# New order of the feed-forward part: x products ahead of c1's, upper halves turned elsewhere, last gate in halves of rows, last norm on ScalarE

## What is computed

```python
x = L0_attn_x
x = _layernorm(x + _L0_attn_ref(x, ...))
x = _layernorm(x + _L0_ffn_ref(x, ...))

def step(c, xt):                       # in _L0_ffn_ref, scanned over the 2 halves of x
    ft = jax.nn.sigmoid(xt @ wf.T + c @ uf.T + bf)
    it = jax.nn.sigmoid(xt @ wi.T + c @ ui.T + bi)
    gt = jnp.tanh(xt @ wc.T + c @ uc.T + bc)
    c = ft * c + it * gt
    return (c, None)
c_final, _ = lax.scan(step, c0, x)
h = jnp.tanh(jnp.einsum('tbi,oi->tbo', x, wo) + c_final @ uo.T + bo)
```

## Time and profile before

| | |
|---|---|
| median of 3 runs | 745.36 us (743.22 to 746.38) |
| the profiled execution | 744.35 us |
| its span | 742.2 us |
| PE busy in the span | 688.9 us (93%) |
| DVE, POOL, ACT busy | 69%, 48%, 44% |
| granted clock of PE over the span | 0.978 |

### The profile page before, as it was taken

One profiled execution on the slowest core, in us unless ns is written; L12 is line 12 of the kernel. 1 busy time (PEld: TensorE's weight loads), 2 busy tenths in 40 slices (PEclk: granted clock), 3 DMA queues, 4 the chain that ended last, 5 costly groups with the idle time before them and its releaser, 6 DMA issues. The chain is left out here.

```text
span 742.2 us, 21921 instructions
## 1 busy us (share of the span) xinstructions
PE 688.9 (93%) x9112; PEld 595.7 (80%) x9112; DVE 509.0 (69%) x1096; ACT 323.0 (44%) x708; POOL 357.0 (48%) x462
## 2 busy tenths in 40 slices
PE   6889999999999999999999999999958889999983
PEld 4778888888888888888888888888846678787872
DVE  3655676878688776867678687968773254575758
ACT  5545445354544344454544445354433233434321
POOL 2645564555646554655655464654541224242415
PEclk9999999999999999999999999999997999999997
DMA  8113031222315030121403041221320000010102
GB/s 282 41 36 91 6 87 27 67 42 50 65 28 91 3 91 9 54 49 45 91 2 90 13 80 35 58 55 25 82 68 0 1 1 14 15 44 15 43 7 93
DMA packets 53586, 37.06 MB, mean 50 GB/s; under 512 B 5360, under 2 KB 52080, under 8 KB 53488
## 3 DMA queue, kind: packets, MB, share of 16 engines
q1 hardware_dynamic: 53488, 35.67, 19.1%
HBM read 30.41 MB, written 5.24 MB: 48 GB/s over the span
## 5 line engine op out<-in xcount | busy, mean ns | idle before, releaser
L365 PE MATMUL bank<-xH,wH 128*128 128x256 f32 x480 | 145.7, 304 | 1.4 <-ACT KT L698 1.4
L365 PE MATMUL bank<-xH,wL 128*128 128x256 f32 x480 | 135.1, 281 | 0.0
L365 PE MATMUL bank<-xL,wH 128*128 128x256 f32 x480 | 135.0, 281 | 0.0
L899 DVE TENSOR_TENSOR W<-bank,E 128x512 f32<-128x512 f32 x128 | 82.2, 684 | 54.9 <-PE bank L365 54.4
L365 PEld LDWEIGHTS bank<-xH,wH 128*128 128x128 f32 x480 | 91.0, 190 | 13.3 <-issue 12.6
L365 PEld LDWEIGHTS bank<-xL,wH 128*128 128x128 f32 x480 | 91.4, 191 | 0.0
L365 PEld LDWEIGHTS bank<-xH,wL 128*128 128x128 f32 x480 | 91.0, 189 | 0.0
L698 ACT ACTIVATE QT<-bank 128x512 f32<-128x512 f32 x64 | 38.2, 596 | 106.0 <-PE bank L365 105.9
L365 PE MATMUL bank<-QT,KT 64*128 64x128 f32 x1024 | 74.4, 285 | 0.0
L698 ACT ACTIVATE E<-bank 128x512 f32<-128x512 f32 x128 | 66.1, 605 | 16.6 <-PE bank L387 16.6
L698 ACT ACTIVATE KT<-bank 128x512 f32<-128x512 f32 x64 | 38.3, 598 | 79.4 <-PE bank L365 79.3
(11 more groups left out here) (150 smaller groups left out, 1700.1 us busy)
## 6 DMA issues: line engine op xcount, KB each, us to landing
cB<-scr SPq DMA_DIRECT2D x240, 64.0 KB, 2.9
xt<-in_xT SPq DMA_DIRECT2D x16, 256.0 KB, 3.2
xs<-in_x SPq DMA_DIRECT2D x16, 256.0 KB, 4.2
out<-xs SPq DMA_DIRECT2D x16, 256.0 KB, 2.1
xt<-in_wffn SPq DMA_DIRECT2D x8, 256.0 KB, 3.0
QT<-in_wqk SPq DMA_DIRECT2D x4, 256.0 KB, 6.2
KT<-in_wqk SPq DMA_DIRECT2D x4, 256.0 KB, 7.3
scr<-cT SPq DMA_DIRECT2D x16, 64.0 KB, 1.9
```

The lines of the kernel that those rows point to most:

```text
L365: return e.matmul(o, a, b, start=start, stop=stop)
L899: return e.tensor_tensor(o, a, b, op)
```

## The change

- The units are cut finer: `("x", blk, t, mt, n)` are the x products of one gate n, `("c", blk, mt, n)` c1's. In the first half of a block (mt = 0) all x products stand ahead of c1's.
- The turn (b, 1) moves: from ahead of gate (b,0,0) to behind gate (b,0,1), directly ahead of the x products of gate (b,1,0). Outputs 4b-4 and 4b-3 stand in and around gate (b,0,1), outputs 4b-2 and 4b-1 among the products of gate (b,1,0). So outputs 8 to 11 are done ahead of the last gate.
- The last gate (3,1,1) is made in two halves of 256 columns (units "h"), in different banks; outputs 12 to 15 have banks of their own.
- An output makes x's products first and c2's after; DVE waits once for both.
- The last norm goes from DVE to ACT as xs*rs3 + nb3, with nb3 = -mean*rs3. For it DVE makes nm3 = -mean (a TENSOR_TENSOR of 128x2 in SBUF) and POOL nb3 (128x2) for each output. One half of output 15 is still normalised on DVE, and its addition of hh to xs goes from POOL to DVE.

```diff
-            units += [u for u in (("g", blk, 1, 0), o(3), ("t", blk + 1, 0), ("g", blk, 1, 1),
-                                  ("t", blk + 1, 1), ("g", blk + 1, 0, 0), o(4), ("g", blk + 1, 0, 1), o(5), o(6)) if u]
-        else:
-            units += [("g", blk, 1, 0), ("g", blk, 1, 1), o(3)]
-    return units + [("o", n) for n in range(12, 18)]
+    out = [[("t", 0, 0), ("t", 0, 1)], g0(0, 0), g0(0, 1)]
+    for blk in range(4):
+        x, c = [[(k, blk) + ((1,) if k == "x" else ()) + (0, n) for n in range(3)] for k in "xc"]
+        if blk == 0:
+            out += [x, c]
+        else:
+            out += [x[0:2] + [("o", 4 * blk - 2)] + x[2:3] + c[0:1] + [("o", 4 * blk - 1)] + c[1:3]]
+        if blk < 3:
+            out += [[("t", blk + 1, 0)], g1(blk), g0(blk + 1, 0)]
+            a = g0(blk + 1, 1)
+            out += [[("o", 4 * blk)] + a[0:2] + [("o", 4 * blk + 1)] + a[2:3], [("t", blk + 1, 1)]]
+    return out + [[("h", h, n) for h in range(2) for n in range(3)], [("o", n) for n in range(12, 18)]]
...
+            def gate_x(blk, t, mt, n):
+                y, idx = blk % 2, 4 * blk + 2 * t + mt
+                if idx >= 2:
+                    e.wait_ge(a_g, 3 * (idx - 2) + n + 1)
...
+                if n == 0:
+                    e.wait_ge(d_y[1], YUSE["t", blk, t] + 1)
...
+            def gate_c(blk, mt, n):
+                y = blk % 2
+                if n == 0 and mt == 0:
+                    e.wait_ge(g_c1l, 2 * blk + 2)
...
+            def gate_h(h, n):
+
+                r = slice(256 * h, 256 * h + 256)
+                e.wait_ge(a_g, 3 * (13 + h) + n + 1)
...
+                if n in (12, 14, 15):
+
+                    e.wait_ge(a_g, 48 if n == 12 else 51)
                 else:
-                    e.wait_ge(a_g, 3 * len(GATE))
-                    e.wait_ge(d_y[1], use - 1)
...
+            def out_norm(n):
+                e.wait_ge(g_rs3, n + 1)
+                for c in (n, n + 16) if n < 15 else (n,):
+                    a = act(xs[:, c, :], xs[:, c, :], ACT.Identity, scale=rs3[:, c:c + 1], bias=nb3[:, c:c + 1])
+                a.then_inc(a_out, 1)
...
+                else:
+                    e.wait_ge(a_hh, n + 1)
+                    dst = xs[:, n:n + 17:16, :]
+                    tt(dst, dst, hh[i][:, :].rearrange("p (t n) -> p t n", t=2), ALU.add).then_inc(d_own, 1)
...
+                e.wait_ge(d_mv3, 3 * n + 2)
+                tt(nm3[:, n:n + 17:16], mv3[:, n:n + 17:16, 0], cs[:, C_NEG:C_NEG + 1].broadcast_to([P, 2]),
+                   ALU.mult).then_inc(d_mv3, 1)
...
-                            root(rs3[:, n:n + 17:16], lr3[:, n:n + 17:16], mv3[:, n:n + 17:16, 1], g_rs3)
+                            e.wait_ge(d_mv3, 3 * n + 3)
+                            r = slice(n, n + 17, 16)
+                            root(rs3[:, r], lr3[:, r], mv3[:, r, 1], g_own)
+                            made += 1
+                            e.wait_ge(g_own, made)
+                            tt(nb3[:, r], nm3[:, r], rs3[:, r], ALU.mult).then_inc(g_rs3, 1)
```

More of the change, by code:

```diff
@@ L179, in program @@
         lr3 = sb("lr3", [P, NC])
+        nm3 = sb("nm3", [P, NC])
+        nb3 = sb("nb3", [P, NC])
         first = ExitStack()
@@ L590, in turn_block @@
                     y.then_inc(p_turn, 1)
[L592 to L616, removed]
-                    m.then_inc(p_gate, 1)
@@ L642, in outputs @@
                                 wH[:, k, wcol(WO)], wL[:, k, wcol(WO)], k == 0, k == 1)
+                m.then_inc(p_o, 1)
+                if blk < 3:
+                    e.wait_ge(g_c2l, 2 * blk + 2)
+                else:
+                    e.wait_ge(d_c2l, 2 if n < 14 else 3)
+                for k in range(2):
+                    m = mm3(Ba[:, 0:256], c2H[y][:, k, c], c2L[y][:, k, c], wH[:, k, wcol(UO)], wL[:, k, wcol(UO)],
+                            k == 0, k == 1)
                 m.then_inc(p_o, 1)
@@ L807, in turn_block, with gate @@
                     act(yH[t][i][:, k, :], turned(blk, k)[:, :], ACT.Copy).then_inc(a_yh, 1)
[L809 to L826, removed]
+            def gate(blk, t, mt, n):
+                y, idx = blk % 2, 4 * blk + 2 * t + mt
+                e.wait_ge(p_gate, 3 * idx + n + 1)
+                if n == 0:
+                    if idx == 0:
+                        e.wait_ge(d_b0, 1)
+                    if blk or t:
+                        p = 2 * blk + mt - (0 if t else 2)
+                        if t:
+                            e.wait_ge(d_c1, 2 * blk + mt + 1)
+                        else:
+                            e.wait_ge(d_c2, p + 1)
+                            e.wait_ge(a_c2, p + 1)
+                            e.wait_ge(g_c2l, p + 1)
+                bias = fvs[:, 3 * mt + n:3 * mt + n + 1] if t else b0[:, mt, n:n + 1]
+                act(gb[mt][n][:, :], ring[mt][n][:, :], ACT.Tanh if n == 2 else ACT.Sigmoid, bias=bias).then_inc(a_g, 1)
+                if n < 2:
+                    return
                 if t == 0:
@@ L884, in _ @@
                 for u in units_at(s):
-                    if u[0] == "g":
-                        gates(*u[1:])
+                    if u[0] == "x" and u[2] == 0:
+                        gate(*u[1:])
+                    elif u[0] == "c":
+                        gate(u[1], 1, *u[2:])
+                    elif u[0] == "h":
+                        gate_h(*u[1:])
                     elif u[0] == "t":
                         turn_block(*u[1:])
-                    elif u[1] < 16:
-                        outputs(u[1])
+                    elif u[0] == "o":
+                        if u[1] < 16:
+                            outputs(u[1])
+                        if 0 <= u[1] - 2 < 16:
+                            out_norm(u[1] - 2)
         @block.vector
@@ L1437, in constants @@
     c[:, C_HALF] = -0.5
+    c[:, C_NEG] = -1.0
     return c
```

155 lines of the change are left out of this document (99 added, 56 removed).

## The result

| | before | changed |
|---|---|---|
| median | 745.36 us | 749.68 us (5 runs, 749.04 to 751.27) |
| ratio | | 1.0065, 95% interval 1.0045 to 1.0085 |
| profiled execution, span | 744.35, 742.2 us | 749.07, 747.3 us |
| PE, DVE, POOL, ACT busy | 93, 69, 48, 44% | 93, 67, 48, 45% |
| granted clock of PE | 0.978 | 0.968 |

The change makes the kernel slower by 0.65%. The shares of busy time hardly move, so the reading goes by stages again. First the rows in which PE's timeline meets a block's end and a wait: the first products of block 1 (in the place of the turn at 604.55 us before), and then, for each block, the wait for yL, the first product behind 12 of 512 and 18 of 256 columns, and the next block's start. Columns as in the earlier trace rows.

The account below looks back on a forecast made before the run. PE was taken to bound the feed-forward part, DVE the stretch from 716.7 us. Terms -6.85, +10.3 and +2.1 gave +5.55 us: 749.9 us profiled, 750.9 us on the median's scale (+0.74%), range 743.5 to 755.5.

Parts of the forecast that it names:

- First part: Gate (0,1,0), x products ahead of c1's: waits of 2.89 and 1.96 us, low clock and restarts go, -6.85 us.
- The three waits: Upper half's turn, three times: PE waits 5.2 us for yL, a 7.4 us chain against 2.2 us of PE work.
- I take 0.37 each as pitch: Two ACT norms of 128x256 in the turn's chain: 0.74 us together, ends 0.54 to 1.10.
- The low clock: Behind each of the three waits for yL PE's clock falls to 1.2 GHz: 1.63 us each, ends nothing and 3.3.
- "36.5" us of work in a block: Steady-state block: PE busy 36.5 us; with 5.2 wait and 1.6 clock 43.3 instead of 38.15, +10.3 for two blocks.
- Tail: Last block and tail: +8.7 up to the last gate's end, then -1.6, -3.6, -1.0 and -0.4, together +2.1 us.
- the period: Tail: hh of outputs 12 to 15 follow at 3.3 us, before 3.6.
- rival 1: Clock stays at 2.4 GHz behind the three waits for yL: 746.0 us, not slower; chance 0.13.
- waits of 1.96 and 2.16 us left it alone: Argument for the clock staying at 2.4 GHz: two waits in the kernel before did not lower it.
- rival 2: nm3 is too small to be blocked by POOL: 747.1 us, within 0.5%; chance 0.13.
- rival 3: Low clock lasts twice as long behind each wait for yL: 755.8 us; chance 0.06.
- The step behind rival 2: nm3 reads two SBUF inputs, so it waits out POOL's addition, about 1.2 us; only 0.32 us per output is gained.

Follow-up runs that it names:

- The run with this part alone: Kernel before, with all three gates' x products ahead of c1's in gate (0,1,0) of block 0: 741.91 us, ratio 0.9954.
- The early turn: Changed kernel with the upper half's turn of block b+1 directly behind the gates of (b,1,1): 727.77 us, ratio 0.9769.
- The filled waits: Changed kernel with 18 discarded matmuls of 512 columns put into each of the three waits for yL: 741.33 us, ratio 0.9945.

## Why the prediction was right, and where its terms were off

**The sum.** Expected 749.9 us for the profiled execution and 750.9 on the median's scale; measured 749.07 and 749.68. By stages the rows give -6.66 (to the end of block 0's gates), +10.55 (blocks 1 and 2: 86.9 us instead of 76.35) and +1.2 (the rest), where the prediction had -6.85, +10.3 and +2.1. That is +5.1 for the span; what lies around the span took 1.8 us instead of 2.15.

**First part.** As predicted: PE waits for nothing between 570 and 597 us, and block 0's gates end at 597.89, predicted 597.7. The run with this part alone gives 4.3 us of it to the wait for c1L.

**The three waits.** Predicted 5.2 each; 4.95, 5.26 and 5.27. The early turn removes them, so their cause is shown. Within the chain one term was mis-sized: "I take 0.37 each as pitch" for a norm on ACT; the two took 0.98 us from start to next start, 0.49 each, in the upper half of my bounds. cu to hh took 0.46 instead of 0.50. From the end of output 5's matmuls to PE's restart the chain took 7.7 us (652.30 to 659.99), not 7.4, but PE's own work ahead of the wait took 2.4, not 2.2 us: the length of the wait came out closer than its parts.

**The low clock was too cheap, and block work too dear; the two cancelled.** I took 1.63 us for each wait. 12 products of 512 and 18 of 256 columns take 4.95 us at full clock (12 at 0.234 and 18 at 0.119 us, the pitches of the run with the early turn); behind the three waits they took 7.33, 7.74 and 6.48 us: 2.4, 2.8 and 1.5 us more, restarts included, in sum 6.7 where I had 4.9. The filled waits agree, 6.8 us. On the other side stood "36.5" us of work in a block, read from PE's busy time. That holds some 1.0 us of slow restarts behind its two waits and of matmuls running out ahead of them, which a busy engine's row counts as work: a block of the change is 43.8 us, less 5.5 from the turn's end to the restart and 2.8 of clock, so 35.5. For blocks 1 and 2 that is 2.0 us too much against 1.9 us of clock too little. That the two cancelled is luck. I should have summed the block from pitches.

**Tail.** From block 3's start to the last gate's end +8.4 by the prediction's 714.3 us, or +8.25 by the start of the next matmul in both kernels, 714.44 and 726.58 us (predicted +8.7); from there to the first hh 3.20 us (3.25); from the first hh to the last 9.30 us against 14.42, -5.1 (-4.6); behind it 8.2 us, -0.4 (-0.4). The mis-sized term is the period, 3.1 and not 3.3 us: nm3 ends 0.02 us behind POOL's addition, L1198, which has 256 elements to do then, 0.16 us behind it. What is missing up to the last gate's end is mostly an old wait: in block 3 of the kernel before PE lost 1.06 us against its pitches, most of it around its wait of 0.47 us, and I had taken off only 0.5. The low clock behind the third wait cost 1.5 us, close to the 1.6 that I had put.

**The rivals.** The clock did not stay at 2.4 GHz: rival 1 falls. What I held for it, that "waits of 1.96 and 2.16 us left it alone", I had read wrongly for the second. In the kernel before PE restarts at 718.91 us behind the wait of 2.16 us; the clock is still 1.00 then and falls 1.5 us later, for some 3 us (columns as for the clock in the profile after):

```profile
719.00:720.00 1.00, 1.00 (x9) 1.00 (x10) 0.91 (x3) 0.09 (x1) 0.00 (x0) 1.00 0.00 0
721.00:722.00 1.00, 1.00 (x7) 1.00 (x6) 1.00 (x2) 0.00 (x0) 1.00 (x2) 0.50 0.00 0
```

So it did behind the wait of 2.18 us near 566 us (0.50 from 567 to 570 us). Of its waits of about 2 us only the one of 1.96 left the clock at 1.00 throughout, and in the run with the last gate in full width one of 1.74 us, shortly behind one of 0.78, did not. These rows give no length of wait that decides. nm3 was blocked in 14 of 16 outputs, the two others being those where POOL does not add: rival 2 falls. The low clock cost 6.7 us, less than twice my 4.9: rival 3 falls. The step behind rival 2 was right for the wrong reason in part. I said nm3 would be blocked because "it reads two inputs from SBUF"; a version with one input was blocked as well, and what frees it is another form of operation.

## What to carry to other kernels

Before a step is moved to just ahead of its reader, add up the chain from its issue to the reader through every engine's queue as it will then stand; here 7.7 us of chain stood against 2.4 us of work, while a place that left 14 us between the turn and its reader (633.2 to 647.3 us in block 2 of that run) cost next to nothing. Price a wait of TensorE with the slow stretch behind it, here 1.5 to 2.8 us on top of 5, and look at the clock for some microseconds behind the restart, since it can fall late. Before a gain is credited to an edit, compare the stretches that were not edited as well. And when a small DVE operation takes a microsecond, look at POOL beside it, and try another form of the operation before moving it to another engine.

## What the runs showed of the hardware

- A DVE operation of two elements a row took 1.05 to 1.29 us beside POOL's addition and 0.16 to 0.17 us without it. Blocked were a TENSOR_TENSOR with two SBUF inputs, a TENSOR_SCALAR with an immediate and, of 128x256, one with two per-row operands (1.29 to 1.32 us); not blocked a TENSOR_REDUCE (0.16 us in all 16 outputs).
- Two waits of the same length (5.26 and 5.27 us) were followed by low clock of 6 and of 3 us; in the run with nm3 on POOL the second, of 5.27 us, had 3. The runs leave open why.
- The clock was low behind waits of 2.16 us (in the kernel before) and of 1.74 us (last gate in full width), falling 1.5 and 0.9 us behind the restart, and not behind one of 1.96 us.
- A wait filled with products that nobody reads, down to 0.66 to 0.98 us of idleness, kept the clock at 2.4 GHz.
- ACT's norm of 128x256 from SBUF to SBUF, with two per-row operands, took 0.59 us (mean of 31) and stood 0.49 us from start to start; the plain copy of that shape took 0.44 us.
